# Attention with the next image's keys and queries placed ahead of the last query chunk, and taps in 8-row pieces

## The chip, the core and the metric

The program runs on one NeuronCore of a Trainium2 chip. The metric is the device time of one execution in microseconds (us). Engines are named as the profile names them: PE (TensorE), DVE (VectorE), ACT (ScalarE), POOL (GpSimd), SP (SyncE, which issues the DMAs).

## What is computed

The input is x, 8 images of 64 channels and 128x128 pixels. Layer 0 is an attention over each image, layer 1 a state-space scan over all images. Only layer 0 is touched by the change. For one image, cut to what matters:

```python
x = mean over 2x2 pixels                      # 64 channels, N = 64*64 = 4096 tokens
gap = mean of x over all tokens;  tg = gap * x
q = tg @ Wq.T + bq;  k = tg @ Wk.T + bk
xK = sigmoid(q) * k + tg                      # the keys
y0, y1 = gelu(5-tap depthwise conv of x, vertical / horizontal), 1x1 conv, scale
xQ = Wh @ concat(y0, y1) + bh                 # the queries
xV = x @ Wo.T + bo                            # the values
attn = softmax(xQ @ xK.T / 8);  z = (attn @ xV) @ Wp.T + bp + xV
zn = layernorm(z)                             # 4096 x 64, then upsampled and given to layer 1
```

## The kernel before

`attention_phase` (lines 69 to 618) writes one instruction stream for each engine; semaphores order them. `mamba_phase` follows and is the same in both kernels. An image has N = 4096 tokens; they are cut into NQ = 8 chunks of TB = 512 queries, and the keys into KT = 32 blocks of 128.

**A query chunk** (PE `chunk`, L555; ACT `exps`, L421; DVE `maxima`, L304 and `normalise`, L318). For each of 32 key blocks PE makes scores `st` from `kf` and `qf` in f32 (L565), ACT takes the exponential into `prob` (L433), and PE adds prob times values into `ob` (L580). Softmax needs the row maximum beforehand, so PE also makes bf16 scores `s` of the *next* chunk in 32 blocks (L530, L531, the `ahead` argument), two in each of the first 16 of the 32 steps, and DVE reduces each with a maximum (L308). At step 18 PE turns the maxima into a row (`max_rows`) and ACT writes that row into partition 64 of `qf` at step 20 (L437), where it is subtracted by the score product itself. After the chunk ACT copies `ob` to `osb` (L443); PE projects it at step 3 of the next chunk (L552), DVE normalises it, with a wait for ACT's `rstd` (step 26 of the next chunk).

**The preparation of an image.** POOL adds 2x2 pixels (L241 to L246) as soon as PE has read the old image for the last time (`v_mm`), then makes the horizontal taps over all 64 rows at once: five products (L261) and four sums (L264), each 64x4096. DVE makes the mean (L354) and the vertical taps, `vertical`, chunk by chunk (L298, L301). When an image's eight chunks are over, ACT makes `tg` (L469, L472), then for each chunk PE makes q and k (L592, L593) and the values (L598), ACT the sigmoid (L456) and the bf16 copy `ka` (L459), DVE the keys (L370, L373), the values (L376) and the rest `ka` (L409). After the last of the eight ACT makes eight gelus (L485) with the query products of PE (L606, 128 rows) and the copies `qf`, `qh` (L490, L493) beside them; DVE sets a row of ones (L385) and makes `qm` (L389). Then PE makes the 32 maxima blocks of chunk 0 by themselves, and only then the first chunk starts.

**Order.** All engines loop over the images. DVE's order within an image (`image`, L360) is keys, `maxima` of chunks 0 and 1, then `mean` and `vertical(0)` of the next image, then for each later chunk `maxima`, `normalise`, `vertical`. SP loads the next image's pixels before it stores this image's chunks.

Of the kernel before, what the change touches and what calls it, by code (L numbers as in the profile page):

```python
# [18 lines left out]
ALU = mybir.AluOpType  # L19
# [4 lines left out]
P = 128  # L24
B, C, H, W = 8, 64, 128, 128
HP, WP = H // 2, W // 2
N = HP * WP
# [27 lines left out]
    ("projb", 64, 1), ("lng", 64, 1), ("lnb", 64, 1), ("cent", 64, 64), ("eps", 128, 1),  # L55
# [13 lines left out]
def attention_phase(nc, x, small, sel, zn):  # L69

    with ExitStack() as ctx:
# [9 lines left out]
        wt = sb("a_small", [P, NCOL])  # L81
# [11 lines left out]
        tg = sb("tg", [P, N])  # L93
        kf = sb("kf", [P, N])
        qf = sb("qf", [P, N])
# [3 lines left out]
        v = sb("v", [P, KT, 2 * C])  # L99
# [85 lines left out]

        block = ctx.enter_context(nc.Block())

        @block.sync
        def _(sp):
            sp.dma_start(wt[:, :], small).then_inc(small_in, 16)  # L190
            sp.wait_ge(zeroed, 3)
# [14 lines left out]
            def store_zn(b):  # L206
                with sp.Fori(0, NQ // 2) as j2:
                    for s in range(2):
                        sp.wait_ge(zn_ready[s], b * (NQ // 2) + j2 + 1)
                        dst = zn[bass.ds(HEAD + b * N + (j2 * 2 + s) * TB, TB), :]  # L210
                        sp.dma_start(dst.rearrange("(q p) c -> p q c", p=P),
                                     znb[s][:, :, :]).then_inc(zn_out[s], 16)

            load_x(0, True)
            with sp.Fori(0, B - 1) as b:
                load_x(b + 1, False)
                store_zn(b)
            store_zn(B - 1)
# [5 lines left out]
        def _(pool):  # L224
            pool.memset(zeros[:, :], 0.0).then_inc(zeroed, 1)
            pool.memset(xb[:, :], 0.0).then_inc(zeroed, 1)
            pool.memset(v[:, :, 2 * C - 1:2 * C], 1.0).then_inc(zeroed, 1)
            pool.wait_ge(zeroed, 3)
            with pool.Fori(0, B) as b:

                pool.wait_ge(tap_h, b * 5)
# [17 lines left out]
                yh = yc[64:128, :].rearrange("p (h w) -> p h w", w=WP)  # L249
# [5 lines left out]
                for k in range(5):  # L255
                    tap = dwq[64:128, k:k + 1].unsqueeze(2).broadcast_to([64, HP, WP])

                    to = yh if k == 0 else yg[64:128, :].rearrange("p (h w) -> p h w", w=WP)
                    if k >= 2:
                        pool.wait_ge(tap_h, b * 5 + k)  # L260
                    pool.tensor_tensor(to, xh[:, :, k:k + WP], tap, ALU.mult).then_inc(tap_h if k == 0 else tap_x, 1)  # L261
                    if k > 0:
                        pool.wait_ge(tap_x, b * 4 + k)
                        pool.tensor_tensor(yh, yh, to, ALU.add).then_inc(tap_h, 1)  # L264

        @block.vector
        def _(dve):
# [50 lines left out]
            def normalise(b, j2, s):  # L318

                g = b * NQ + j2 * 2 + s  # L320
# [3 lines left out]
                for qb in range(4):  # L324
                    vq = v[:, bass.ds((j2 * 2 + s) * 4 + qb, 1), 0:C].rearrange("p a c -> p (a c)")
                    dve.scalar_tensor_tensor(z[:, qb, :], zt[:, qb, 0:C], rden[:, qb:qb + 1], vq,
                                             ALU.mult, ALU.add).then_inc(z_step, 1)
# [32 lines left out]
            def image(b, more):  # L360

                for ch in range(NQ):
# [10 lines left out]
                    dve.tensor_tensor(kf[:, cols], kb[:, :], tg[:, cols], ALU.add).then_inc(kf_done, 1)  # L373

                    dve.wait_ge(v_mm, g + 1)
                    dve.tensor_tensor(v[:, ch * 4:ch * 4 + 4, 0:2 * C - 1],  # L376
# [4 lines left out]
                    if ch > 0:  # L381
                        middle(g - 1, ch - 1)
                middle(b * NQ + NQ - 1, NQ - 1)
                dve.wait_ge(ka_done, (b + 1) * NQ)
                dve.memset(kf[64:65, :], 1.0).then_inc(krow, 1)  # L385
                for ch in range(NQ):
                    cols = slice(ch * TB, ch * TB + TB)
                    dve.wait_ge(qh_done, b * NQ + ch + 1)
                    dve.tensor_tensor(qm[:, cols], qf[:, cols], qh[:, cols], ALU.subtract).then_inc(qm_done, 1)  # L389
                maxima(b * NQ)  # L390
                maxima(b * NQ + 1)
                if more:
                    mean(b + 1)
                    vertical(b + 1, 0)
                with dve.Fori(0, NQ // 2 - 1) as j2:
                    for s in range(2):
                        maxima(b * NQ + j2 * 2 + s + 2)
                        normalise(b, j2, s)
                        if more:
                            vertical(b + 1, j2 * 2 + s + 1)  # L400
                if more:
                    vertical(b + 1, NQ - 1)
                normalise(b, NQ // 2 - 1, 0)
                normalise(b, NQ // 2 - 1, 1)

            def middle(g, ch):
                cols = slice(ch * TB, ch * TB + TB)
                dve.wait_ge(kh_done, g + 1)
                dve.tensor_tensor(ka[64:128, cols], kf[64:128, cols], ka[64:128, cols],  # L409
                                  ALU.subtract).then_inc(ka_done, 1)  # L410
# [4 lines left out]
            with dve.Fori(0, B - 1) as b:  # L415
                image(b, True)
            image(B - 1, False)

        @block.scalar
        def _(act):  # L420
            def exps(g, next_cols, rest):  # L421

                for t in range(KT):
                    if t == MAX_ROW_T and next_cols is not None:
                        max_row(g + 1, next_cols)
# [9 lines left out]
            def max_row(g, cols):  # L435
                act.wait_ge(mrow_mm, g + 1)
                act.mul(qf[64:65, cols], rb[0:1, :], -1.0).then_inc(mrow_done, 1)  # L437
# [13 lines left out]
            def keys(b, ch):  # L451
# [5 lines left out]
                if ch > 0:  # L457
                    act.wait_ge(kf_done, g)
                    act.copy(ka[:, (ch - 1) * TB:ch * TB], kf[:, (ch - 1) * TB:ch * TB]).then_inc(kh_done, 1)  # L459

            act.wait_ge(small_in, 16)
            with act.Fori(0, B) as b:
                act.wait_ge(gap_v, b * 3 + 3)
                for ch in range(NQ):
                    g = b * NQ + ch
                    cols = slice(ch * TB, ch * TB + TB)
                    rows = slice(ch * 8, ch * 8 + 8)

                    act.activation(tg[0:64, cols].rearrange("p (h w) -> p h w", w=WP),  # L469
                                   xv[:, 2 + ch * 8:10 + ch * 8, :], ACT.Copy,  # L470
                                   scale=gapf[0:64, :]).then_inc(tg_ready, 1)
                    act.activation(tg[64:128, cols].rearrange("p (h w) -> p h w", w=WP),  # L472
                                   xh[:, rows, 2:2 + WP], ACT.Copy, scale=gapf[64:128, :]).then_inc(tg_ready, 1)
                    if ch > 0:
                        keys(b, ch - 1)
                keys(b, NQ - 1)
                act.wait_ge(kf_done, b * NQ + NQ)
                act.copy(ka[:, N - TB:N], kf[:, N - TB:N]).then_inc(kh_done, 1)
                act.wait_ge(tap_v, (b + 1) * NQ * 5)
                act.wait_ge(tap_h, (b + 1) * 5)  # L480
                act.wait_ge(setup_v, 14)
                for ch in range(NQ + 1):
                    if ch < NQ:
                        cols = slice(ch * TB, ch * TB + TB)
                        act.activation(yg[:, cols], yc[:, cols], ACT.Gelu, bias=w("bdw")).then_inc(gelu_done, 1)  # L485
                    if ch > 0:
                        k = ch - 1
                        cols = slice(k * TB, k * TB + TB)
                        act.wait_ge(ph_mm, b * NQ + k + 1)
                        act.activation(qf[:, cols], s1[k % 2][:, :], ACT.Identity, bias=bqq[:, 0:1])\  # L490
                           .then_inc(qf_done[k % 2], 1)
                        act.wait_ge(qf_done[k % 2], b * (NQ // 2) + k // 2 + 1)
                        act.copy(qh[:, cols], qf[:, cols]).then_inc(qh_done, 1)  # L493
                act.preload_act_table_set(LN_EXP)
                act.wait_ge(qm_done, (b + 1) * NQ)
                max_row(b * NQ, slice(0, TB))
                exps(b * NQ, slice(TB, 2 * TB), False)
                outputs(b * NQ)
                with act.Fori(1, NQ - 1) as j:
                    g = b * NQ + j  # L500
                    exps(g, bass.ds((j + 1) * TB, TB), True)
                    outputs(g)
                g = b * NQ + NQ - 1
                exps(g, None, True)
                outputs(g)
                rstds(g)

        @block.tensor
        def _(pe):
# [15 lines left out]
            def score_block(t, j):  # L525
# [7 lines left out]
            def maxima_blocks(g, j, t):  # L533

                pe.wait_ge(s1_max, g * 32 + t - 1) if t >= 2 else pe.wait_ge(s1_max, g * 32)
                score_block(t, j)
# [798 lines left out]
```

## Time and profile before

| | us |
|---|---|
| median of 3 runs (12467.69 to 12474.12) | 12469.56 |
| the profiled execution | 12465.74 |
| its span, first to last instruction | 12463.9 |
| PE busy in the span | 11440.9 (92%) |
| DVE busy | 9896.2 (79%) |
| ACT busy | 7888.2 (63%) |
| POOL busy | 7860.5 (63%) |

The profiled execution is the one from which all durations here are taken; it lies 3.8 us below the median. The shares are averages over two layers with different limits, so they do not say what bounds the attention. The attention takes the first 4893 us or so; stages of it are read from windows of the trace.

### The profile page before, as it was taken

To read this page: it belongs to the slowest core of one execution; us is meant where nothing else is said; L and a number is where in the kernel's file an instruction comes from. 1 tells how busy PE (TensorE), PEld (TensorE's weight loads), DVE (VectorE), ACT (ScalarE), POOL (GpSimd) and SP (SyncE) were. 2 spreads that over 40 slices of the span, in tenths; PEclk is the share of its full clock that TensorE was granted. 3 is DMA by queue.
4 is the path that set the end of the run, shared out by engine and by line. 5 is a ranking of instruction groups with operands and counts; after the bars stand their busy time and mean duration, and the time that the engine had idled before them with its cause. 6 is when DMAs were issued, how large, how long until landed. Compare 5 with 4: busy or idle time off the path is not lost.

```text
span 12463.9 us, 161217 instructions
## 1 busy us (share of the span) xinstructions
PE 11440.9 (92%) x33768; PEld 4251.5 (34%) x33768; DVE 9896.2 (79%) x12696; ACT 7888.2 (63%) x12821; POOL 7860.5 (63%) x5925
## 2 busy tenths in 40 slices
PE   4989898989899999999999999999999999999998
PEld 1333333333333333333333333333333333333333
DVE  6454545454536344999999999999999999999999
ACT  2333333333333334888888888888888888888888
POOL 6030303030303001999999999999999999999999
PEclk9989898989899999999999999999999999999999
DMA  2010101010100001444444444444444444444444
GB/s 59 2 29 2 28 2 29 2 28 2 29 9 21 3 1 52 174 185 173 180 184 171 183 181 173 185 178 176 185 174 179 185 171 183 182 172 185 179 175 186
DMA packets 408439, 1433.35 MB, mean 115 GB/s; under 512 B 180242, under 2 KB 180370, under 8 KB 267926
## 3 DMA queue, kind: packets, MB, share of 16 engines
q1 hardware_dynamic: 408342, 1432.48, 30.9%
q14 instruction: 88, 0.72, 0.0%
q8 instruction: 9, 0.15, 0.0%
HBM read 1380.68 MB, written 51.62 MB: 115 GB/s over the span
## 4 chain that ended last, share of the span: by engine, by line
DVE 22%; issue 22%; PE 7%; ACT 4%; POOL 3%; DVEq 2%; POOLq 0%; ACTq 0%; DMA 0%; SPq 0%
DVE bbank L940 10%; DVE h L961 9%; POOL e L837 3%; PE vbank L1144 2%; PE vbank L1143 2%; PE ybank L1195 2%; DVE qn L930 1%; ACT L1018 1%; ACT sz L1015 1%; PE ubank L1147 1%; PE bbank L1185 1%; ACT da L1085 1%; ACT so L1053 1%; DVE dl L919 1%; DVE yb L926 1%
## 5 line engine op out<-in xcount | busy, mean ns | idle before, releaser
L871 POOL TENSOR_TENSOR pr<-h,cc 128x512 f32<-128x512 f32 x4109 | 5157.1, 1271 | 543.8 <-DVE h L961 543.6
L961 DVE TENSOR_TENSOR_SCAN h<-da,h,bbank 128x512 f32<-128x512 f32 x3596 | 4497.4, 1261 | 0.0
L1195 PE MATMUL ybank<-pr,m_small 128*128 128x512 f32 x8212 | 4141.5, 595 | 0.3 <-POOL pr L871 0.3
L433 ACT ACTIVATE prob<-st 128x512 f32<-128x512 f32 x2048 | 1222.7, 597 | 2573.5 <-PE st L565 2573.5
L1085 ACT ACTIVATE da<-dl,a 128x512 f32<-128x512 f32 x3599 | 2445.4, 713 | 148.4 <-DVE dl L919 138.4
L940 DVE TENSOR_TENSOR bbank<-bbank,du 128x512 f32<-128x512 f32 x3597 | 2415.7, 672 | 4.4 <-POOL du L841 2.1
L308 DVE TENSOR_REDUCE mpart<-s 128x1 f32<-128x512 f32 x2048 | 1321.4, 686 | 1089.7 <-PE s L531 1081.6
L565 PE MATMUL st<-qf,kf 65*128 (+1 forms) x4096 | 2121.1, 620 | 5.9 <-ACT qf L437 5.9
L241 POOL TENSOR_TENSOR rowsum<-xin 128x1024 f32<-128x1024 f32 x64 | 154.0, 2406 | 2994.2 <-PE vb L598 2905.9
L1185 PE MATMUL bbank<-bcs,selb 96*128 96x512 bf16 x3598 | 1387.3, 386 | 474.4 <-DVE h L961 464.2
L1195 PEld LDWEIGHTS ybank<-pr,m_small 128*128 128x128 f32 x8212 | 1519.4, 191 | 829.7 <-POOL pr L871 378.5
L1185 PEld LDWEIGHTS bbank<-bcs,selb 96*128 96x128 bf16 x3598 | 345.4, 96 | 2192.3 <-DVE h L961 1790.5
L580 PE MATMUL ob<-prob,v 128*64 128x512 f32 x4096 | 1090.6, 616 | 0.0
L565 PEld LDWEIGHTS st<-qf,kf 65*128 65x128 f32 x4096 | 696.3, 190 | 1123.0 <-issue 617.7
L832 POOL TENSOR_TENSOR ed<-ed,av 128x512 f32<-128x512 f32 x258 | 328.7, 1274 | 1034.2 <-ACT ed L1037 1034.2
L530 PE MATMUL s<-ka,qh 128*128 128x512 bf16 x2048 | 791.7, 387 | 132.9 <-DVE mpart L308 109.5
L531 PE MATMUL s<-ka,qm 128*128 128x512 bf16 x2048 | 787.6, 385 | 0.0
L338 DVE TENSOR_SCALAR zn<-z,mv,rstd 128x64 f32<-128x64 f32 x256 | 62.9, 310 | 912.5 <-ACT rstd L449 912.5
L961 DVE TENSOR_TENSOR_SCAN h<-bbank,h,dbp 128x512 f32<-128x512 f32 x513 | 651.9, 1271 | 56.6 <-ACT bbank L1085 56.6
L860 POOL TENSOR_TENSOR dbp<-cc,du 128x512 f32<-128x512 f32 x514 | 653.7, 1272 | 3.3 <-DMA cc<-c_rows 3.3
L1010 ACT ACT_TABLE_LOAD x258 | 331.0, 1283 | 479.2 <-PE vbank L1144 477.0
L301 DVE SCALAR_TENSOR_TENSOR yc<-xb,dwq,yc (+1 forms) x256 | 455.4, 1779 | 33.3 <-DVE yc L301 23.4
(156 smaller groups left out, 12201.2 us busy)
## 6 DMA issues: line engine op xcount, KB each, us to landing
cc<-c_rows SPq DMA_DIRECT2D x1032, 1024.0 KB, 8.0
cc<-c_rows SPq DMA_DIRECT2D x258, 512.0 KB, 11.5
upw<-up SPq DMA_DIRECT2D x260, 256.0 KB, 10.3
xin<-x SPq DMA_DIRECT2D x128, 512.0 KB, 6.7
out<-ot SPq DMA_DIRECT2D x256, 128.0 KB, 2.3
zw<-zn_tokens SPq DMA_DIRECT2D x780, 32.0 KB, 10.5
c_rows<-crows SPq DMA_DIRECT2D x258, 36.0 KB
zn_tokens<-znb SPq DMA_DIRECT2D x64, 128.0 KB, 2.0
```

What stands on the lines that cost most here:

```text
L308: dve.tensor_reduce(mpart[:, t:t + 1], s1[t % 2][:, :], AX.X, ALU.max).then_inc(s1_max, 1)
L433: act.activation(prob[t % 4][:, :], st[t % 2][:, :], ACT.Exp).then_inc(exp_done, 1)
L530: pe.matmul(s1[t % 2][:, :], qh[:, q], keys, start=True, stop=False)
L531: pe.matmul(s1[t % 2][:, :], qm[:, q], keys, start=False, stop=True).then_inc(s1_mm, 1)
L565: pe.matmul(st[t % 2][:, :], kf[0:C + 1, t * P:t * P + P], q, start=True, stop=True).then_inc(st_mm, 1)
L580: mm = pe.matmul(ob[64 * half:64 * half + 64, :], v[:, k + half, C:2 * C], prob[(k + half) % 4][:, :], start=(k == 0), stop=(k == KT - 2))
L871: pool.tensor_tensor(pr[:, n % 8, :], h[:, n, :], cc[par][:, n, :], ALU.mult).then_inc(prod_done, 1)
L940: dve.tensor_tensor(bbank[n % 4][:, :], bbank[n % 4][:, :], du[par][:, :], ALU.mult)\
L961: dve.tensor_tensor_scan(h[:, n, :], decay, inp, h[:, n, TB - 1:TB], ALU.mult, ALU.add).then_inc(scan_done, 1)
L1085: act.activation(to, dl[par][:, :], ACT.Exp, scale=a[:, n:n + 1]).then_inc(da_done, 1)
L1185: pe.matmul(bbank[n % 4][:, :], selb[:, n, :], bcs[par][:, :], start=True, stop=True)\
L1195: pe.matmul(ybank[:, :], w("ident"), pr[:, n % 8, :], start=False, stop=(n == S - 1))\
```

## The change

The image loop is turned by one stage. The keys, values and queries of image b+1 are made between chunk 6 and chunk 7 of image b, and chunk 7 carries the maxima of the next image's chunk 0, which it had none of before. What chunk 7 still reads is kept: two buffers each for the keys (`kt`, which also holds `tg`: the sum is made in place), the values (`vv`) and the last chunk's queries (`qlast`). `tg` is made in chunks 2 to 5, two pieces behind each (`scaled`). All eight gelus come first, then keys and queries chunk by chunk. The query product goes into `ob` instead of `s`. POOL's taps are made in eight pieces of 8 rows (64x512 each). DVE's `mean` comes after the normalising of chunk 0 and the vertical taps follow in chunks 2 to 6, at most two chunks of taps at a time. SP stores six chunks, loads the image after the next, and stores the other two. The load of the small operands leaves out the columns that only layer 1 uses. The last image has no preparation, and its chunk 7 no maxima.

```diff
+        kt = [sb(f"kt{i}", [P, N]) for i in range(2)]
+        qlast = [sb(f"qlast{i}", [P, TB]) for i in range(2)]
+        vv = [sb(f"vv{i}", [P, KT, 2 * C]) for i in range(2)]
...
@block.sync
+            with sp.Fori(0, B - 2) as b:
+                store_zn(b, range(NQ - 2))
+                load_x(b + 2, False)
+                store_zn(b, range(NQ - 2, NQ))
...
@block.gpsimd
+                for ch in range(NQ):
+                    part = slice(ch * TB, ch * TB + TB)
...
+                    for k in range(5):
+                        tap = dwq[64:128, k:k + 1].unsqueeze(2).broadcast_to([64, 8, WP])
...
+                        pool.tensor_tensor(to, xh[:, ch * 8:ch * 8 + 8, k:k + WP], tap, ALU.mult)\
+                            .then_inc(tap_h if k == 0 else tap_x, 1)
+                        if k > 0:
+                            pool.wait_ge(tap_x, (b * NQ + ch) * 4 + k)
+                            pool.tensor_tensor(yh, yh, to, ALU.add).then_inc(tap_h, 1)
...
@block.vector
+            def keys_queries(b, p):
...
                     if ch > 0:
+                        middle(g - 1, p, ch - 1)
+                        query_rest(b, p, ch - 1)
+                middle(b * NQ + NQ - 1, p, NQ - 1)
                 dve.wait_ge(ka_done, (b + 1) * NQ)
                 dve.memset(kf[64:65, :], 1.0).then_inc(krow, 1)
+                query_rest(b, p, NQ - 1)
...
+            def batch(b, p, first, more):
                 maxima(b * NQ + 1)
+                if not first:
+                    normalise(b - 1, 1 - p, NQ - 1)
+                taps = {1: (0, 1), 2: (2, 3), 3: (4, 5), 4: (6,), 5: (7,)}
+                for j in range(NQ - 2):
+                    maxima(b * NQ + j + 2)
+                    normalise(b, p, j)
+                    if more and j == 0:
+                        mean(b + 1)
+                    if more:
+                        for ch in taps.get(j, ()):
+                            vertical(b + 1, ch)
                 if more:
+                    keys_queries(b + 1, 1 - p)
+                    maxima(b * NQ + NQ)
+                normalise(b, p, NQ - 2)
...
@block.scalar
+            def keys_queries(b, p):
+                act.wait_ge(tap_v, (b + 1) * NQ * 5)
+                act.wait_ge(tap_h, (b + 1) * 5 * NQ)
...
+                for ch in range(NQ):
+                    cols = slice(ch * TB, ch * TB + TB)
+                    act.activation(yg[:, cols], yc[:, cols], ACT.Gelu, bias=w("bdw")).then_inc(gelu_done, 1)
+                for ch in range(NQ):
+                    keys(b, p, ch)
+                    cols = slice(ch * TB, ch * TB + TB)
+                    act.wait_ge(ph_mm, b * NQ + ch + 1)
+                    act.activation(queries(p, ch), ob[:, :], ACT.Identity, bias=bqq[:, 0:1])\
+                       .then_inc(qf_done[ch % 2], 1)
+                    act.wait_ge(qf_done[ch % 2], b * (NQ // 2) + ch // 2 + 1)
+                    act.copy(qh[:, cols], queries(p, ch)).then_inc(qh_done, 1)
+                round_keys(b, p, NQ - 1)
+                act.preload_act_table_set(LN_EXP)
...
+                with act.Fori(2, NQ - 2) as j:
+                    exps(b * NQ + j, qf[64:65, bass.ds((j + 1) * TB, TB)], True)
+                    outputs(b * NQ + j)
+                    if more:
+                        for half in range(2):
+                            scaled(1 - p, j * 2 + (half - 4))
+                exps(g + NQ - 2, qlast[p][64:65, :], True)
+                outputs(g + NQ - 2)
+                if more:
+                    keys_queries(b + 1, 1 - p)
+                    act.wait_ge(qm_done, (b + 2) * NQ)
+                exps(g + NQ - 1, qf[64:65, 0:TB] if more else None, True)
+                outputs(g + NQ - 1)
...
@block.tensor
+            def chunk(g, p, q, ahead, behind, fresh=None):
                 pe.wait_ge(mrow_done, g + 1)
+                if fresh is not None:
+                    pe.wait_ge(sig_done, fresh * NQ + NQ)
...
+                    if fresh is not None and t == 1:
+                        pe.wait_ge(qm_done, fresh * NQ + NQ)
+                        pe.wait_ge(krow, fresh + 1)
+                        pe.wait_ge(v_done, fresh * NQ + NQ)
+                    first = 0 if fresh is None else 2
+                    if ahead is not None and first <= t < KT // 2 + first:
...
+            def keys_queries(b, p, behind):
                 for ch in range(NQ):
...
                     mm.then_inc(v_mm, 1)
+                    pe.wait_ge(gelu_done, b * NQ + ch + 1)
...
+                        pe.wait_ge(qf_done[(ch - 1) % 2], b * (NQ // 2) + (ch - 1) // 2 + 1)
+                    pe.matmul(ob[:, :], wc[:, :], yg[:, ch * TB:ch * TB + TB], start=True,
                               stop=True).then_inc(ph_mm, 1)
...
+            with pe.Fori(0, (B - 2) // 2) as b2:
+                for s in range(2):
+                    batch(b2 * 2 + s + 1, 1 - s, False, True)
```

## Rows read from the trace of the kernel before

**Rows 1.** Windows: us, then busy of PE, PEld, DVE, ACT, POOL; PEclk, DMA, GB/s.

```profile
633.70:696.00 62.30, 62.30 (x209) 21.94 (x210) 31.67 (x65) 20.68 (x37) 0.00 (x0) 1.00 0.01 2
696.00:743.30 47.30, 47.29 (x136) 14.91 (x136) 3.77 (x19) 20.05 (x35) 0.00 (x0) 1.00 0.01 3
743.30:839.70 96.40, 74.08 (x192) 32.82 (x192) 62.03 (x96) 41.67 (x64) 33.33 (x22) 0.70 0.40 89
901.90:978.80 76.90, 64.27 (x209) 22.31 (x210) 42.97 (x62) 20.64 (x36) 14.07 (x2) 0.91 0.01 2
```

**Rows 2.** Timeline of ACT: start us, us, engine, line, operation, count, idle before.

```profile
244.98 0.58 ACT L437 ACTIVATE qf<-rb 1x512 f32<-1x512 f32 x1 [25.43 <-PE rb L542]
...
839.68 0.58 ACT L437 ACTIVATE qf<-rb 1x512 f32<-1x512 f32 x1 [25.24 <-PE rb L542]
...
4409.73 0.58 ACT L437 ACTIVATE qf<-rb 1x512 f32<-1x512 f32 x1 [24.60 <-PE rb L542]
```

**Rows 3.** Timeline: POOL and DVE while POOL makes the second image's taps; then PE.

```profile
858.04 8.84 POOL L264 TENSOR_TENSOR yc<-yc,yg 64x4096 f32<-64x4096 f32 x1
...
883.21 33.38 DVE L301 SCALAR_TENSOR_TENSOR yc<-xb,dwq,yc 64x512 f32<-64x512 f32 x4
...
692.82 3.08 DVE L301 SCALAR_TENSOR_TENSOR yc<-xb,dwq,yc 64x512 f32<-64x512 f32 x4
...
917.25 0.61 PE L530 MATMUL s<-ka,qh 128*128 128x512 bf16 x1 [12.63 <-DVE mpart L308]
```

**Rows 4.** Timeline of PE between two images: q and k products of consecutive chunks.

```profile
753.35 2.04 PE L592 MATMUL st<-tg,a_small 64*128 64x512 f32 x2 [8.20 <-ACT tg L472]
...
768.84 1.91 PE L592 MATMUL st<-tg,a_small 64*128 64x512 f32 x2
...
773.96 1.91 PE L592 MATMUL st<-tg,a_small 64*128 64x512 f32 x2
```

**Rows 5.** Windows, columns as in Rows 1: keys, query products (two windows), chunk 1 after its stall.

```profile
760.00:795.00 35.00, 34.65 (x83) 20.51 (x81) 18.66 (x27) 15.53 (x25) 0.00 (x0) 0.50 0.06 14
797.30:801.30 4.00, 3.75 (x4) 1.14 (x4) 3.09 (x3) 2.40 (x5) 3.63 (x4) 0.50 0.00 0
801.50:813.00 11.50, 6.57 (x12) 1.74 (x12) 9.42 (x8) 11.27 (x19) 8.01 (x6) 1.00 0.82 182
917.20:921.00 3.80, 3.75 (x7) 1.36 (x8) 1.97 (x3) 0.12 (x1) 0.00 (x0) 0.50 0.00 0
921.00:925.00 4.00, 4.00 (x22) 2.21 (x20) 2.73 (x5) 1.07 (x2) 0.00 (x0) 1.00 0.01 2
```

**Rows 6.** Groups by line, 743.3 to 839.7 us: busy us, mean ns, idle before.

```profile
L485 ACT ACTIVATE yg<-yc,a_small 128x512 f32<-128x512 f32 x8 | 5.6, 717 | 0.0
L373 DVE TENSOR_TENSOR kf<-kb,tg 128x512 f32<-128x512 f32 x8 | 5.5, 692 | 0.3
L456 ACT ACTIVATE sg<-st,a_small 128x512 f32<-128x512 f32 x8 | 5.5, 687 | 18.4 <-PE st L592 18.4
...
L490 ACT ACTIVATE qf<-s,bqq 128x512 f32<-128x512 f32 x8 | 5.4, 672 | 1.6 <-PE s L606 1.6
...
L493 ACT CAST qh<-qf 128x512 bf16<-128x512 f32 x8 | 4.9, 618 | 0.3
...
L385 DVE MEMSET kf<- 1x4096 f32 x1 | 3.5, 3472 | 0.9 <-DVE ka L409 0.9
...
L469 ACT ACT_TABLE_LOAD x1 | 1.3, 1283 | 2.5 <-issue 2.5
```

**Rows 7.** Timeline of DVE at the end of the keys, POOL busy with the next image.

```profile
795.40 4.31 DVE L409 TENSOR_TENSOR ka<-kf,ka 64x512 bf16<-64x512 f32 x2
```

**Rows 8.** Taps of the first image in POOL's timeline; POOL's 128x512 form on the page.

```profile
66.24 7.01 POOL L261 TENSOR_TENSOR yc<-xb,dwq 64x4096 f32<-64x4096 f32 x1
...
80.58 9.13 POOL L264 TENSOR_TENSOR yc<-yc,yg 64x4096 f32<-64x4096 f32 x1
...
L871 POOL TENSOR_TENSOR pr<-h,cc 128x512 f32<-128x512 f32 x4109 | 5157.1, 1271 | 543.8 <-DVE h L961 543.6
```

More of the change, by code:

```diff
@@ L226, in _ @@
             pool.memset(xb[:, :], 0.0).then_inc(zeroed, 1)
[L227 to L228 removed]
+            for i in range(2):
+                pool.memset(vv[i][:, :, 2 * C - 1:2 * C], 1.0).then_inc(zeroed, 1)
+            pool.wait_ge(zeroed, 4)
             with pool.Fori(0, B) as b:
[L231 removed]
+                pool.wait_ge(tap_h, b * 5 * NQ)
                 pool.wait_ge(v_mm, b * NQ)
@@ L254, in _ @@
                 pool.wait_ge(setup_v, 4)
[L255 to L264, printed above, removed]
+                for ch in range(NQ):
+                    part = slice(ch * TB, ch * TB + TB)
+                    yh = yc[64:128, part].rearrange("p (h w) -> p h w", w=WP)
+                    yx = yg[64:128, part].rearrange("p (h w) -> p h w", w=WP)
+                    for k in range(5):
+                        tap = dwq[64:128, k:k + 1].unsqueeze(2).broadcast_to([64, 8, WP])
+                        to = yh if k == 0 else yx
+                        if k >= 2:
+                            pool.wait_ge(tap_h, (b * NQ + ch) * 5 + k)
+                        pool.tensor_tensor(to, xh[:, ch * 8:ch * 8 + 8, k:k + WP], tap, ALU.mult)\
[3 more added lines that the diff above has]
+                            pool.tensor_tensor(yh, yh, to, ALU.add).then_inc(tap_h, 1)
         @block.vector
@@ L358, in mean @@
                                       ALU.mult).then_inc(gap_v, 1)
-            def image(b, more):
+            def keys_queries(b, p):
+                kf = kt[p]
                 for ch in range(NQ):
@@ L390, in image @@
-                maxima(b * NQ)
-                maxima(b * NQ + 1)
-                if more:
[L393 to L402, printed above, removed]
@@ L414, in _, with exps @@
                 vertical(0, ch)
-            with dve.Fori(0, B - 1) as b:
-                image(b, True)
-            image(B - 1, False)
+            keys_queries(0, 0)
+            maxima(0)
+            batch(0, 0, True, True)
+            with dve.Fori(0, (B - 2) // 2) as b2:
+                for s in range(2):
+                    batch(b2 * 2 + s + 1, 1 - s, False, True)
+            batch(B - 1, 1, False, False)
+            normalise(B - 1, 1, NQ - 1)
         @block.scalar
         def _(act):
-            def exps(g, next_cols, rest):
+            def exps(g, next_row, rest, at=MAX_ROW_T):
                 for t in range(KT):
-                    if t == MAX_ROW_T and next_cols is not None:
-                        max_row(g + 1, next_cols)
+                    if t == at and next_row is not None:
+                        max_row(g + 1, next_row)
                     if t == KT - 6 and rest:
@@ new lines, in _ @@
+            act.wait_ge(small_in, 16)
+            act.wait_ge(gap_v, 3)
+            for ch in range(NQ):
+                scaled(0, ch)
+            keys_queries(0, 0)
+            act.wait_ge(qm_done, NQ)
+            max_row(0, qf[64:65, 0:TB])
+            batch(0, 0, True, True)
+            with act.Fori(0, (B - 2) // 2) as b2:
+                for s in range(2):
+                    batch(b2 * 2 + s + 1, 1 - s, False, True)
+            batch(B - 1, 1, False, False)
+            rstds(B * NQ - 1)
```

199 lines of the change are left out of this document (86 added, 113 removed), and 2 rows, old and new, of the table LAYOUT.

## Prediction

> **What bounds the kernel now.** I read the windows first, stage by stage, because the page's shares mix two layers. In a middle chunk PE is busy for the whole 62.3 us at full clock, with ACT at 20.7 and DVE at 31.7: PE bounds it. Chunk 7, which carries no maxima, takes 47.3. Two stretches fall out of this pattern: the 96.4 us between two images, where PE shows 74 us at a mean clock of 0.70, and chunk 1, which takes 76.9 for the same work [rows 1]. Then the marks on ACT: the first and the last image's first maximum row stand at 244.98 and 4409.73, so a period is 4164.75 / 7 = 594.96 us [rows 2]. Eight chunks of 62.28 (62.30 in the window) would be 498.24; **96.72 us of each period are something else**: 96.4 between images, 14.6 lost in chunk 1 (76.9 less 62.3), less the 15.0 that the short chunk 7 saves [rows 1]; chunk 1 varies a little from image to image.
>
> Why chunk 1 is long: POOL's tap passes last 8.84 us each, and four vertical taps of DVE that take 3.08 by themselves take 33.38 beside them, so the next maxima are late and PE stands for 12.63 us [rows 3]. Why the preparation is slow: after 8.2 us of idle, q to next q is 773.96 - 768.84 = 5.12 us [rows 4], with PE busy 34.65 of 35 us at 0.50, that is 1.2 GHz [rows 5]. So three products (q, k, values) of 5.12 / 3 = 1.71 us each set the pace, and ACT and DVE, at 15.5 and 18.7 of the 35 us, have time to spare.
>
> **The change part by part.**
>
> *Mean and vertical taps move* behind chunk 1, when POOL's taps are long over: POOL starts pooling after the last value product of the stage, ahead of chunk 7, needs some 50 us, then about 105 for the taps (below), and is done early in chunk 1. The 15 us of chunk 1 go. Two chunks of taps take 2 x 4 us after the normalising (3.08 for four of the five instructions [rows 3]); they end about when the next chunk starts, and its first maximum is wanted 1.5 us later: nothing.
>
> *tg moves* into chunks 2 to 5, four copies of 0.72 (as a gelu [rows 6]), about 3.0 us in front of the next chunk's exponentials. PE has two steps (some 3.5 us, from the pace of chunk 1's first steps) before it needs the first of them; ACT is through with it after osb 0.6, the four copies and 0.6 for itself, 4.3 with hops. I take 1.0 us x 4 = **4.0** (0, if PE's steps are slower, to 12, if nothing hides them).
>
> *The stage* stays in line on PE: chunk 7 is issued behind it, so it is not hidden, only rearranged. From the end of chunk 6 [durations: rows 6]:
> 1. osb 0.6, table load 1.28, eight gelus (5.6 busy, overlapping a little) 5.4, table load 1.28, sigmoid 0.69: 9.3.
> 2. keys and values on DVE, three at 0.7 and hops of 0.2: 2.7. Only then may PE write the second chunk's values. PE has nothing to do for 6 us before that, and 8.2 us of idle ended at half clock, so I take half clock from here.
> 3. values and query product of chunk 1: 3.4.
> 4. six turns of q, k, v and query product, 4 x 1.71 = 6.83 us: 41.0. ACT has 2.6 us of work in a turn (sigmoid, ka, qf, qh) and DVE 3.5 (five at 0.7); PE sets it.
> 5. The tail, now in the open: qf 0.67, qh 0.62, ka 0.62, rest of ka 0.69, row of ones 3.47, qm 0.69, six hops 1.2: 8.0. POOL begins to pool beside it; two rests of ka took 4.31 there instead of 1.4 [rows 7], so I add 2.9 once (0 to 6): 10.9.
>
> Sum 67.3, less the 1.1 us (osb and a hop) that lies there in any chunk: **66.2**. Chunk 7 then runs with the maxima, 62.28 (counted). Its start is at half clock: after the stall of chunk 1, PE was at 0.50 for 3.8 us, then at 1.00 [rows 5], so 1.8 lost. The maxima end two steps later, close to the row that uses them: 0.7. The two normalisings beside POOL's taps: 1.0, mostly hidden (0 to 8, below).
> Total 66.2 + 4.0 + 1.8 + 0.7 + 1.0 = 73.7 against 96.72: 23.0 less in each of seven periods, **-161 us**.
>
> *Taps in pieces.* A 64x512 piece is bounded below by an eighth of 7.01 and 8.84 (0.88 and 1.1) [rows 3, 8] and above by POOL's two-tensor 128x512 form, 1.27 [rows 8]; I take 1.03 and 1.25 with hops of 0.1: 90 us an image instead of 72. For images 1 to 7 this hides behind chunks. For the first it does not: DVE gets in between two pieces, which costs POOL 0.3 each time (9.13 against 8.84 [rows 3, 8]), 12 for 40 taps. From 66.24 [rows 8] the taps end at 168; the stage without osb takes 66.7, and the lone maxima of image 0 stay, 25.2 (the idle time before the row at 839.68 [rows 2]): first row at 260 instead of 244.98 [rows 2], **+15**. Bounds: -15 if pieces cost an eighth and DVE fits for nothing, +31 if each costs 1.27 and DVE 0.5.
>
> *Loop ends.* ACT stood 2.5 us with no releaser at the image loop's end [rows 6]; that is in the 96.4, and now the loop runs three times with two images each: **+4** (0 to 8). *Smaller small-operand load, split stores on SP*: nothing; the pixels arrive during chunk 7 and are wanted a period later, and the two stores now queued behind the load wait for POOL's pooling, 50 us from the end of the stage, while the first of them is ready only at the end of chunk 7. On POOL nothing but the next image is queued behind the pieces. On PE the new waits hold all of chunk 7; that is the tail above.
>
> -161 + 15 + 4 = -142: 12465.7 - 142 = 12324 for the profiled execution, 3.8 more for the median: **12327**.
>
> **The rivals.**
> *The clock rises within the stage (0.30).* The rows speak both ways. Dense q, k and v products, 64 rows each, stayed at 0.50 for 35 us; the 128-row query products ended that: four passes at 0.50 up to 801.3, and 1.00 behind them with PE busy only 6.57 of 11.5 us [rows 5]. In the new turn a quarter of PE's time is such a product. At full clock PE needs 3.4 us a turn and DVE's five instructions with hops, 4.2, set it: 2.6 saved in up to six turns of eight stages, -126, so down to 12200. The Trainium skill (TensorE: Matmul & The Clock Gate, Part 1) has it that a PE kept busy is let up to 2.4 GHz; by that rule this rival would hold, and the old keys would have run at 1.00. The measured 0.50 over 35 busy us speaks against the rule for 64-row work, so I hold the other case likelier.
>
> *DVE still waits on POOL (0.08).* POOL's 72 pieces now lie under chunk 7 and chunk 0 instead of chunks 0 and 1. Of two normalisings, twelve instructions could each wait for a piece of 1.27: 15 us a period, of which half has no slack behind it: 7 x 7 = +50, 12377. The Trainium skill (SBUF — State Buffer, Who interferes with whom) lets a DVE instruction with two SBUF inputs and a POOL one that reads SBUF exclude each other for a whole instruction. By that rule the wait would hit them; the taps agree (33.38 against 3.08 [rows 3]), and no row shows a normalising beside POOL.
>
> *Nothing gained (0.03).* A turn is set by the handing over between PE, ACT and DVE and takes 9.0 us: 2.2 more in each of 8 turns of 8 stages, 141, which eats the saving: 12468.
>
> *Slower (0.04): chunk 7 stays at half clock.* Its score products have 65 rows, near those which did not raise the clock. A chunk in which PE is busy throughout takes twice its 62.28 at half: 7 x 60 = +420, some 12750; it decides from 46 us at half clock on (23 lost). Against it: chunk 1 came back in 3.8 us [rows 5], with maxima blocks in it as chunk 7 now has.
>
> **How the numbers follow.** Half clock in the stage 0.55, clock up 0.30, the rest 0.15. The forecast is the likeliest's. Its own range is 12290 to 12365 (first image, POOL's waits, hand-overs). Low end: the clock rises from the second turn on and the first image gains, 12190. High end: DVE waits and the first image at its worst, 12395. A measurement of this kernel can tell about 0.2% (25 us) from no change; the first three cases lie beyond that: faster 0.93, same 0.03, slower 0.04.
>
> **What would show it.** Right: chunk 1 at 62.3 us; period near 572; copies of chunk 6 to first exponential of chunk 7 near 67, with PE at 0.50 and q to q 6.8; chunk 7 near 65; first row near 260. Wrong in a step: q to q near 4.2 (clock); a PE wait on maxima in chunk 0 or 7 (DVE behind POOL); PEclk of 0.50 beyond 5 us of chunk 7; ACT table loads among the exponentials of chunks 2 to 5.

## Result and profile after

The changed kernel takes 12329.1 us (median of 4 runs, 12328.55 to 12330.39) against 12468.76 before (12467.69 to 12474.12): a ratio of 0.9887, 95% interval 0.987 to 0.9904. The profiled execution took 12328.55 with a span of 12326.7, 137.2 less than the one before. The forecast was 12327 with a range of 12190 to 12395.

The page barely moves: PE goes from 11440.9 us of busy time to this (busy us, share of the span, instructions, by engine).

```profile
PE 11430.3 (93%) x33578; PEld 4269.2 (35%) x33768; DVE 9659.4 (78%) x12696; ACT 7881.3 (64%) x12814; POOL 7945.5 (64%) x6430
```

By these records PE lost only 10.6 us of work (190 matmuls fewer are recorded than the chunks and stages issue, so this is rough); most of the gain is idle time that went. To see where, the next rows mark the stages: ACT's timeline (start, us, engine, line, operation, count, idle before) with the gelus' table load in the first image, the first maximum row, the copy `osb` after chunk 0 of the first image, two marks of the second image's stage, and the copy after chunk 0 of the last.

```profile
164.50 1.28 ACT L505 ACT_TABLE_LOAD   x1 [79.87 <-issue]
...
258.77 0.58 ACT L463 ACTIVATE qf<-rb 1x512 f32<-1x512 f32 x1 [31.96 <-PE rb L588]
...
320.97 0.58 ACT L469 COPY osb<-ob 128x512 f32<-128x512 f32 x1 [1.28 <-PE ob L632]
...
1270.61 0.59 ACT L469 COPY osb<-ob 128x512 f32<-128x512 f32 x1 [1.28 <-PE ob L632]
...
1340.06 1.08 ACT L459 ACTIVATE prob<-st 128x512 f32<-128x512 f32 x2 [6.54 <-DVE qm L406]
...
4338.28 0.58 ACT L469 COPY osb<-ob 128x512 f32<-128x512 f32 x1 [1.28 <-PE ob L632]
```

The first row comes at 258.77 instead of 244.98 [rows 2]: 13.8 us **lost** in the first image. From 320.97 to 4338.28 lie seven periods: 573.90 us each instead of 594.96, so 7 x 21.06 = 147.4 **gained**. That is 133.6 in the attention. The last 3.5 lie in layer 1, which is the same code: from the last copy `osb` to the end it took 7570.9 before and 7567.4 here, and 7575.7 in the run with only the taps in pieces, below; it differs by so much between executions.

The 64 copies `osb` cut a period into chunks. Chunk 1 is 62.28 instead of some 77; the four chunks that start behind `tg` copies (3 to 6) are 63.07; chunk 7 with the stage in front of it is 133.5 in the mean (133.85 in the first six, 131.3 in the last, beside which POOL has no further image to pool); two chunk 0, of the fourth and the sixth image, are 66.8, where the image loop jumps back. Windows of a middle chunk (chunk 1 of the third image), the second image's stage, its six turns alone, and chunk 7's start (us, then busy of PE, PEld, DVE, ACT, POOL, with counts; PEclk, DMA, GB/s):

```profile
1466.90:1529.20 62.30, 62.13 (x206) 21.94 (x210) 29.56 (x58) 20.68 (x37) 0.00 (x0) 1.00 0.01 3
1270.60:1342.00 71.40, 59.06 (x118) 28.52 (x119) 35.00 (x41) 30.31 (x46) 9.68 (x6) 0.56 0.15 32
1281.80:1330.10 48.30, 48.30 (x94) 24.23 (x95) 23.94 (x34) 15.01 (x25) 1.05 (x1) 0.50 0.00 0
1342.00:1346.00 4.00, 3.78 (x7) 1.26 (x7) 1.38 (x2) 0.60 (x1) 3.67 (x3) 0.50 0.87 195
1346.00:1350.00 4.00, 4.00 (x19) 2.05 (x18) 1.29 (x2) 0.60 (x1) 3.17 (x3) 0.85 0.49 113
```

In chunk 1 PE is busy for 62.13 of 62.30 us at full clock, as in any middle chunk; in the stage its mean clock is 0.56. The third row is the heart of the stage: PE busy for all of 48.30 us at 0.50, as the old keys were [rows 5]. One turn of it in PE's timeline, q to q:

```profile
1281.76 2.04 PE L651 MATMUL vb<-woq,xb 64*128 64x127 f32 x8 [5.37 <-DVE vv L390]
...
1285.74 2.07 PE L645 MATMUL st<-kt,a_small 64*128 64x512 f32 x2
1287.61 1.91 PE L646 MATMUL s<-kt,a_small 64*128 64x512 f32 x2
1289.31 1.91 PE L651 MATMUL vb<-woq,xb 64*128 64x127 f32 x8
1291.15 2.08 PE L661 MATMUL ob<-yg,wc 128*128 128x512 f32 x2
1293.16 2.07 PE L645 MATMUL st<-kt,a_small 64*128 64x512 f32 x2
...
1330.12 3.62 PE L612 MATMUL st<-qlast,kt 65*128 65x512 f32 x4
1340.71 2.07 PE L612 MATMUL st<-qlast,kt 65*128 65x512 f32 x2 [6.97 <-ACT prob L459]
```

A turn is 1293.16 - 1285.74 = 7.42 us. From start to start, q takes 1.87, k 1.70, the values 1.84 and the query product (128 rows, between products of 64) 2.01. The stage's tail and the normalising beside POOL's pieces, in DVE's timeline:

```profile
1329.08 2.86 DVE L430 TENSOR_TENSOR ka<-kt,ka 64x512 bf16<-64x512 f32 x1
...
1335.75 3.47 DVE L400 MEMSET kt<- 1x4096 f32 x1 [0.91 <-DVE ka L430]
1339.25 0.69 DVE L406 TENSOR_TENSOR qm<-qlast,qh 128x512 bf16<-128x512 f32 x1
...
1395.09 2.66 DVE L351 TENSOR_SCALAR zn<-z,mv,rstd 128x64 f32<-128x64 f32 x4 [10.94 <-ACT rstd L475]
1397.79 1.53 DVE L354 TENSOR_TENSOR zn<-zn,a_small 128x256 f32<-128x256 f32 x1
1399.45 1.05 DVE L359 TENSOR_TENSOR znb<-zn,a_small 128x256 f32<-128x256 f32 x1
...
1406.07 1.29 DVE L320 TENSOR_REDUCE mpart<-s 128x1 f32<-128x512 f32 x2 [5.56 <-PE s L577]
```

Two of POOL's groups by line (busy us, mean ns, idle) are the taps' sums and products of the second to the eighth image (250 to 4900 us):

```profile
L276 POOL TENSOR_TENSOR yc<-yc,yg 64x512 f32<-64x512 f32 x224 | 283.5, 1266 | 17.6
L272 POOL TENSOR_TENSOR yg<-xb,dwq 64x512 f32<-64x512 f32 x224 | 235.3, 1050 | 13.2
```

One rest of `ka` takes 2.86 instead of 0.69 beside POOL's pooling; the row of ones and `qm` keep their 3.47 and 0.69. The normalising is slower beside the pieces (by itself it takes 0.98, 0.43 and 0.43: 3.4 us more), but DVE waits 5.56 us for PE behind it, so it costs nothing.

### The profile page after: what moved, and what is told of

Read it like the earlier page. It is cut to its first block, busy times and chain, and to the rows that moved or that the text cites. A ratio compares the mean times of both kernels' runs of the same rounds, so it can differ in the third digit from the quotient of the medians.

```text
span 12326.7 us, 160391 instructions
## 1 busy us (share of the span) xinstructions
PE 11430.3 (93%) x33578; PEld 4269.2 (35%) x33768; DVE 9659.4 (78%) x12696; ACT 7881.3 (64%) x12814; POOL 7945.5 (64%) x6430
## 4 chain that ended last, share of the span: by engine, by line
DVE 23%; issue 22%; PE 7%; ACT 4%; POOL 3%; DVEq 2%; POOLq 0%; ACTq 0%; DMA 0%; SPq 0%
DVE bbank L1008 11%; DVE h L1029 9%; POOL e L905 3%; PE vbank L1212 2%; PE vbank L1211 2%; PE ybank L1263 2%; DVE qn L998 1%; ACT L1086 1%; ACT sz L1083 1%; PE ubank L1215 1%; PE bbank L1253 1%; ACT da L1153 1%; ACT so L1121 1%; DVE dl L987 1%; DVE yb L994 1%
## 5 line engine op out<-in xcount | busy, mean ns | idle before, releaser
L612 PE MATMUL st<-qf,kt 65*128 (+1 forms) x3584 | 1865.2, 620 | 20.8 <-ACT prob L459 14.6
L632 PE MATMUL ob<-prob,vv 128*64 128x512 f32 x4096 | 1090.5, 616 | 0.0
L612 PEld LDWEIGHTS st<-qf,kt 65*128 65x128 f32 x3584 | 605.8, 189 | 985.3 <-issue 556.6
L576 PE MATMUL s<-ka,qh 128*128 128x512 bf16 x1858 | 709.9, 382 | 2.6 <-DVE mpart L320 2.6
L632 PEld LDWEIGHTS ob<-prob,vv 128*64 128x64 f32 x4096 | 207.9, 134 | 592.3 <-ACT prob L459 536.5
```

Source lines behind the costliest of these rows:

```text
L576: pe.matmul(s1[t % 2][:, :], qh[:, q], keys, start=True, stop=False)
L612: pe.matmul(st[t % 2][:, :], kt[p][0:C + 1, t * P:t * P + P], q, start=True, stop=True).then_inc(st_mm, 1)
L632: mm = pe.matmul(ob[64 * half:64 * half + 64, :], vv[p][:, k + half, C:2 * C], prob[(k + half) % 4][:, :], start=(k == 0), stop=(k == KT - 2))
```

## The experiments

Each diff is cut to the lines that carry the edit.

**1. Which edit removes chunk 1's stall?** Two went with the change: the taps' new place and their cut into pieces. Each was put into the kernel before by itself.

```diff
-                if more:
-                    mean(b + 1)
-                    vertical(b + 1, 0)
...
+                taps = {1: (0, 1), 2: (2, 3), 3: (4, 5), 4: (6,), 5: (7,)}
...
+                    if more and j == 0:
+                        mean(b + 1)
+                    if more:
+                        for ch in taps.get(j, ()):
+                            vertical(b + 1, ch)
```

> The kernel before, with DVE's mean and vertical taps moved behind the normalising of chunk 0 and spread over chunks 2 to 6 as in the changed kernel; nothing else. Theory (chunk 1 is long because DVE sits in a tap behind POOL's 8.8 us passes): chunk 1 falls from 77 to 62.3 in seven images, 7 x 14.9 = 104 less: about 12364, and the time between images stays 96.4. Rival (the turned loop, not the taps, carries the gain): the wait moves to a later chunk, within 25 us of 12469.

Measured: 12360.91, ratio 0.9914 (0.9898 to 0.9931). Chunk 1 is 62.28 in all images; the rest is as before.

```diff
+                for ch in range(NQ):
+                    part = slice(ch * TB, ch * TB + TB)
...
+                            pool.tensor_tensor(yh, yh, to, ALU.add).then_inc(tap_h, 1)
```

> The kernel before, with only POOL's taps cut into 64x512 pieces. Theory: a vertical tap waits for one piece of 1.3 us instead of a pass of 8.8, five of them take some 10 us and end before the first maxima of chunk 1 are wanted, so chunk 1 is 62.3: -104. In the first image DVE's taps end near 132 us instead of 165, the keys follow, and the first row comes near 213 instead of 245: -32. Together about 12333, as fast as the changed kernel with its turned loop. Rival (the turned loop carries the gain): pieces still block DVE in chunk 1 or lengthen POOL's work, 12440 to 12480.

Measured: 12328.05, ratio 0.9888 (0.9871 to 0.9904): **as fast as the whole change**, with the image loop unturned. In its timeline, the first maximum row on ACT, then DVE's taps and maxima beside POOL's pieces:

```profile
214.62 0.59 ACT L441 ACTIVATE qf<-rb 1x512 f32<-1x512 f32 x1 [25.69 <-PE rb L546]
...
836.35 1.08 DVE L302 TENSOR_SCALAR yc<-xb,dwq 64x512 f32<-64x512 f32 x1
837.47 6.21 DVE L305 SCALAR_TENSOR_TENSOR yc<-xb,dwq,yc 64x512 f32<-64x512 f32 x4
858.29 1.29 DVE L312 TENSOR_REDUCE mpart<-s 128x1 f32<-128x512 f32 x2 [14.61 <-PE s L535]
```

Four vertical taps take 6.21 instead of 33.38 [rows 3], and it is now DVE that waits 14.61 us for PE. Either edit alone takes the stall away. Only the pieces also help the first image: its row comes at 214.62 instead of 244.98 [rows 2], in the first edit at 245.72.

The period of the pieces alone is 580.1 us ((4337.74 - 276.82) / 7 between the copies after chunk 0). So turning the loop is worth 580.1 - 573.9 = 6.2 x 7 = 43 us, and it gives back 258.8 - 214.6 = 44 in the first image: there, keys now come behind the gelus, which wait for all taps, where before keys were made while the taps ran.

**2. The other way round: whole passes in the turned loop.**

```diff
-                for ch in range(NQ):
-                    part = slice(ch * TB, ch * TB + TB)
...
+                for k in range(5):
+                    tap = dwq[64:128, k:k + 1].unsqueeze(2).broadcast_to([64, HP, WP])
```

> The changed kernel with POOL's taps again in whole passes of 64x4096 (8.8 us). Theory (a normalising that falls beside POOL's taps waits for a pass with each instruction that has two SBUF inputs or runs in the fast mode): the normalisings in chunk 7 and chunk 0 take up to 50 us instead of 2, the next maxima are late, chunk 0 or 1 grows by 20 to 40 us in seven images: 12470 to 12610, with a PE wait on maxima. The first image: taps end near 165 as with pieces. Rival (normalising does not meet the taps, only the old place of the vertical taps did): no chunk grows, 12315 to 12335.

Measured: 12447.2 (one run), 118 above the change. Chunk 0 grows to 82 to 84 us in six images. DVE's timeline in one of them, from 1420 us on (so the first line has three of its four operations), then the wait of PE there (waiter, releaser; us, count, longest):

```profile
1419.89 7.46 DVE L347 TENSOR_SCALAR zn<-z,mv,rstd 128x64 f32<-128x64 f32 x3
1427.38 8.91 DVE L350 TENSOR_TENSOR zn<-zn,a_small 128x256 f32<-128x256 f32 x1
1436.43 7.13 DVE L355 TENSOR_TENSOR znb<-zn,a_small 128x256 f32<-128x256 f32 x1
```

```profile
PE s L572 <- DVE mpart L316: 17.9, 1, 17.9
```

One product of the normalising takes 8.91 us, a whole pass of POOL (8.84 [rows 3]), instead of 1.53 beside pieces, and PE waits 17.9 for the maxima behind it. So the pieces are what makes the turned order possible; with whole passes the stall only moves from chunk 1 to chunk 0. The theory had the direction right and the size too large. The Trainium skill (SBUF — State Buffer, Who interferes with whom) says of such a pair of DVE and POOL instructions that one locks the other out for its whole length; this row agrees, where the trace before had no normalising beside POOL.

The first image's first maximum row in this run, in ACT's timeline, comes as late as with pieces (258.77):

```profile
257.63 0.59 ACT L459 ACTIVATE qf<-rb 1x512 f32<-1x512 f32 x1 [31.52 <-PE rb L584]
```

**3. Does the number of rows hold the clock down in the stage?** The products of q, k and values were given 128 rows instead of 64, with zeros in the lower half of the weights: the columns and the sums stay the same.

```diff
-        woq = sb("woq", [64, 2 * C - 1])
+        woq = sb("woq", [P, 2 * C - 1])
...
+            dve.memset(woq[64:128, :], 0.0)
...
-                    pe.matmul(st[ch % 2][:, :], w("wqT"), kt[p][0:64, cols], start=True, stop=True).then_inc(q_mm, 1)
+                    pe.matmul(st[ch % 2][:, :], full("wqT"), kt[p][:, cols], start=True, stop=True).then_inc(q_mm, 1)
```

> The changed kernel with the q, k and value products made on all 128 rows: the weights' lower 64 rows are zero, so the sums are the same and the columns streamed are the same. Theory (64-row work, however dense, does not bring the clock up): PE goes to 1.00 within some 10 us of the stage, a turn falls from 7.4 to 4.2 to 5 us (set by DVE), 12 to 18 us less in each of eight stages and chunk 7 starts warm: 12170 to 12240. Rival (what keeps the clock down is the waits between the products, not their rows): PEclk stays 0.50 in the stage and the turn at 6.8 to 7.4: 12300 to 12335; it falls to 6.8 if the 0.6 beyond four products is the change between 64 and 128 rows.

Measured: **12146.61**, ratio 0.9743 (0.9727 to 0.976). Windows of the second image's stage, columns as above, then PE's timeline: the last query product at half clock, two turns, and chunk 7:

```profile
1236.70:1240.50 3.80, 3.78 (x11) 2.77 (x12) 2.86 (x5) 0.09 (x1) 0.00 (x0) 0.50 0.00 0
1240.50:1262.00 21.50, 21.50 (x86) 12.50 (x86) 19.38 (x29) 14.97 (x25) 0.74 (x1) 1.00 0.00 1
```

```profile
1238.56 1.92 PE L663 MATMUL ob<-yg,wc 128*128 128x512 f32 x2
1240.27 1.17 PE L647 MATMUL st<-kt,a_small 128*128 128x512 f32 x2
...
1243.88 1.02 PE L647 MATMUL st<-kt,a_small 128*128 128x512 f32 x2
...
1247.35 1.02 PE L647 MATMUL st<-kt,a_small 128*128 128x512 f32 x2
...
1272.93 2.07 PE L614 MATMUL st<-qlast,kt 65*128 65x512 f32 x2 [9.82 <-ACT prob L461]
```

After 3.8 us at 0.50 the granted clock is 1.00, and a turn takes 3.47 us instead of 7.42. PE busy throughout was not enough: the same products on 64 rows stayed at 0.50 for 48.3 busy us. The stage with chunk 7 is some 111 us instead of 133.5 (7 x 22.7 = 159), and the first row comes at 236.40 (22 earlier); together 181 of the 182.5 gained. It went below the theory's range, since DVE, busy 19.38 of 21.5 us, still keeps up with PE at 3.47 a turn. The tail is now the longest wait: PE stands for 9.82 us behind chunk 7's first two blocks of scores. At half clock, too, a product is shorter where its neighbours have 128 rows: the query product takes 1240.27 - 1238.56 = 1.71 us from its start to the next, against 2.01 between products of 64 rows.

The same edit in the unturned kernel of experiment 1 with the pieces:

> The kernel before with two edits: taps in pieces, and q, k and value products on 128 rows; the image loop is not turned. Theory (the clock is what the old preparation lost; the turned loop is worth little by itself): a turn of the keys falls from 5.1 us to about 3 (DVE's four instructions), 8 turns of 8 images, 135 less than pieces alone: 12180 to 12210. The difference to the changed kernel with 128 rows (12147) is then what turning the loop is worth once the clock is up, 35 to 60. Rival (turning the loop is worth nothing even then): 12140 to 12155. Rival (the clock stays down here, since the stage starts after 8 us of idle): 12320 to 12335.

Measured: 12223.68, ratio 0.9801 (0.9784 to 0.9819), 104 less than the pieces alone, and 14 above the theory's range. Its keys in windows:

```profile
706.00:710.00 4.00, 2.22 (x3) 1.17 (x4) 0.00 (x0) 3.02 (x6) 0.00 (x0) 0.50 0.77 169
...
714.00:718.00 4.00, 4.00 (x18) 2.33 (x17) 2.62 (x5) 3.44 (x6) 0.00 (x0) 1.00 0.68 145
```

So at half clock the turned loop is worth nothing over the pieces (12329.1 against 12328.05), and at full clock 77 us (12146.61 against 12223.68). By the traces, the seven periods gain 7 x 13.14 = 92 at full clock (551.14 against 564.28) where they gained 43 at half clock, and the first image gives back 22 (236.40 against 214.59) instead of 44; the other 7 lie in layer 1, the same code. The clock helps the new order more: it takes 3.95 us off a turn, which holds the query product too, but only 2.29 off a turn of the old order (5.12 to 2.83).

**4. The smaller terms.** Each run undoes one of the costs that the forecast listed.

The row of ones made chunk by chunk, ahead of the tail:

```diff
                         query_rest(b, p, ch - 1)
+                        ones(b, p, ch - 1)
...
-                dve.wait_ge(ka_done, (b + 1) * NQ)
-                dve.memset(kf[64:65, :], 1.0).then_inc(krow, 1)
```

> The changed kernel with the row of ones written chunk by chunk (1x512, eight times) behind each chunk's rest of the query, instead of once (1x4096) at the end of the stage. Theory (the tail of the stage is a chain on DVE, and 3.5 us of ones with the 0.9 us in front are part of it): first exponential of chunk 7 some 4.4 us sooner in eight stages, 35 less: about 12294. Rival (the tail is held by POOL's pooling, which DVE meets whatever it does): no more than 10 less, 12318 to 12330.

Measured: 12310.08 (ratio 0.9871, 0.9853 to 0.9888), in between: 19 us. In the trace a period falls by 3.09 (573.90 to 570.81), of the 3.47 that the memset takes. The tail in DVE's timeline:

```profile
1323.87 2.86 DVE L434 TENSOR_TENSOR ka<-kt,ka 64x512 bf16<-64x512 f32 x1
...
1329.66 2.72 DVE L410 TENSOR_TENSOR qm<-qlast,qh 128x512 bf16<-128x512 f32 x1
```

The rest of `ka` takes 2.86 as before, but the last `qm` now 2.72 instead of 0.69: without the memset ahead of it, it falls beside POOL's pooling, which takes part of the gain back.

The `tg` copies between the exponentials instead of behind them:

```diff
-                    if more:
-                        for half in range(2):
-                            scaled(1 - p, j * 2 + (half - 4))
+                    exps(b * NQ + j, qf[64:65, bass.ds((j + 1) * TB, TB)], True, after=after)
```

> The changed kernel with the four copies of tg put between exponentials of the second half of the chunk (after steps 21, 23, 27, 29), where ACT waits for PE 1.5 us in every two steps, instead of behind the chunk. Theory (the 0.79 us that chunks 3 to 6 grew are these copies in front of the next chunk's exponentials): chunks 3 to 6 go back to 62.28, 7 x 4 x 0.79 = 22 less: about 12307. Rival (ACT's gap is too short for a copy of 0.72 with its hops): the copies delay exponentials, 12325 to 12360.

Measured: 12309.43, ratio 0.9869 (0.9852 to 0.9887). All four chunks are back at 62.28: the copies' cost was 0.79 x 4 x 7 = 22 us.

The image loop written out on PE, ACT and DVE:

```diff
-            with pe.Fori(0, (B - 2) // 2) as b2:
+            for b2 in range((B - 2) // 2):
```

> The changed kernel with the loop over pairs of images written out on PE, ACT and DVE. Theory (the two periods in which chunk 0 took 66.8 instead of 62.3 are the loop's two jumps back): both fall to 62.3, 9 less: about 12320. Rival (they come from elsewhere, such as the order of stores and loads): no change, 12326 to 12331; or longer, where more code has to be fetched.

Measured: 12323.32, ratio 0.9881 (0.9863 to 0.9898). Both chunks of 66.8 are 62.28.

The first image's keys ahead of its gelus, as in the kernel before:

```diff
+                if apart:
+                    for ch in range(NQ):
+                        keys(b, p, ch)
+                    round_keys(b, p, NQ - 1)
                 act.wait_ge(tap_v, (b + 1) * NQ * 5)
```

> The changed kernel with one difference in the first image alone: its keys and values are made before its gelus and queries, while POOL still makes the taps (the old order), instead of side by side behind the last tap. Theory (the 43 us that the turned loop gains in seven periods are given back in the first image, where nothing runs beside the preparation): first row near 215 instead of 258.8, as with pieces in the old loop, so 12285 to 12295. Rival (the first image is held by POOL's taps and the lone maxima in either order): 12315 to 12330.

Measured: 12293.73, ratio 0.986 (0.9844 to 0.9876), 35 less. The first row in ACT's timeline shows where it came from, 222.98 against 258.77:

```profile
222.98 0.58 ACT L465 ACTIVATE qf<-rb 1x512 f32<-1x512 f32 x1 [24.96 <-PE rb L602]
```

**5. Together.** Products on 128 rows, `tg` between the exponentials, the loop written out (on POOL too), and the row of ones by POOL, chunk by chunk, ahead of its pooling (DVE also makes the last `qm` ahead of the last rest of `ka`):

```diff
+                for ch in range(NQ):
+                    pool.wait_ge(ka_done, b * NQ + ch + 1)
+                    pool.memset(kt[b % 2][64:65, ch * TB:ch * TB + TB], 1.0).then_inc(krow, 1)
```

> The changed kernel with q, k, values on 128 rows, tg inside the chunk, the image pairs written out, and the row of ones made by POOL chunk by chunk ahead of its pooling, so that neither the ones nor the pooling lies beside DVE's tail. Theory (the costs are separate): from 12147, -22 for tg, -6 for the loop, and the tail from 11 us to 4 or 5, 6 less in eight stages, -48, with some more where chunk 7 starts warm: 12055 to 12080. Rival (with the clock up the tail is held elsewhere, by ACT's copies or the table load): 12100 to 12120.

Measured: 12059.89, ratio 0.9672 (0.9656 to 0.9688). The stage with chunk 7 falls from 111 to 103.3. A window of chunk 7's start shows what is left there, the clock below full again:

```profile
1249.00:1253.00 4.00, 4.00 (x13) 1.76 (x11) 1.94 (x3) 0.60 (x1) 3.79 (x3) 0.60 0.18 27
```

With the first image's keys ahead of its gelus as well (the edits of both runs):

> The kernel of e11_all with the first image's keys and values made before its gelus, as in e10_first_apart. Theory: with the clock up the side by side stage is shorter, so less is given back in the first image than in e10_first_apart: 20 to 30 less than e11_all. Rival (no gain, since with the clock up the order does not matter): within 8 of e11_all.

Measured: **12053.08**, ratio 0.9666 (0.965 to 0.9683), the fastest of all: 276 us below the change and 415 below the kernel before. The last edit is worth 7 here and 35 by itself: the 20 to 30 expected did not come, and the rival held. Once the clock is up, the first image's keys behind its taps are short. The first row stands at 223.52, no earlier than without the full clock (222.98), since POOL's taps hold it in both. The table load ahead of the first gelu waits for the last of them, here and in the run with only the first image changed:

```profile
170.59 1.28 ACT L537 ACT_TABLE_LOAD   x1 [14.38 <-POOL yc L286]
```

```profile
170.80 1.28 ACT L519 ACT_TABLE_LOAD   x1 [3.66 <-POOL yc L276]
```

## Why the prediction was right, and where it was off

The total holds: -142 was forecast for the profiled execution and -137.2 measured. Half clock, the case taken at 0.55, is what happened. Point by point:

- *Chunk 1's stall goes*: right, 62.28. The text gave the new place of the taps as the reason. The runs show that the pieces alone do it too, and that in the new order the place needs the pieces.
- *The stage, 67.3*: measured 69.45, from 1270.61 to 1340.06. To the sigmoid's end 8.9 (9.3), to the second values 2.25 (2.7), to the next q 3.98 (3.4), six turns 1330.12 - 1285.74 = 44.4 (41.0), tail 9.94 (10.9). **The term that failed is the turn**: "4 x 1.71 = 6.83" priced all four products as the old three [rows 4], and it took 7.42. The extra 0.6 lies at the change between products of 64 and of 128 rows: in the run where all have 128 rows, the query product takes 1.71 at the same half clock instead of 2.01, and four products take 3.47 at full clock, twice which is 6.94. A whole turn without the change was not measured at half clock.
- *The tail*: POOL beside it costs 133.85 - 131.3 = 2.5, against 2.9.
- *Chunk 7's start*: the second image's stage with chunk 7 takes 133.98. A chunk is 62.28 of it and the stage without its `osb` 68.35 (69.45 - 1.1), so 3.3 is lost, against 1.8 + 0.7 (and 1.0 for the normalising, which cost nothing). PE stayed below full clock until after 1346.
- *`tg` copies*: 0.79 a chunk for 1.0. *Loop ends*: two jumps of 4.5, 9 for 4.
- *First image*: +13.8 for +15, with taps that ended at 164.5 for 168 (pieces of 1.05 and 1.27 us in the later images, for 1.03 and 1.25). The sum puts the whole stage behind the taps, which is what happened. But +15 and its bounds were told as the price of slower taps on POOL. That was the wrong cause: with whole passes in the turned loop the row is as late, at 257.63, and the pieces alone brought it *forward* by 30 us. The later row comes from the keys' place behind the gelus, worth 35 in its own run.

Summed: the periods gave 147.4 where 161 less the loop's 4, or 157, was forecast, 9.6 short: 5 from the loop, the rest from the turn's 7 x 3.4 = 24 less what most other terms of the stage came out cheaper. The first image came 1.2 cheaper and layer 1 varied by 3.5, which leaves 4.9, the difference of 142 and 137.2. So it is in part luck that the median lies within 2 us of the forecast: the errors nearly cancel.

Of the rivals: the clock did not rise, and the third experiment shows that the 64 rows kept it down, as the forecast held likelier. The price of that rival was too small: in that run the clock rose and 12146.61 was measured, below the range's 12190, since DVE's five instructions take 3.47 us a turn and not 4.2. By the rule of the Trainium skill (TensorE: Matmul & The Clock Gate, Part 1), that a PE kept busy goes to full speed, 48.3 busy us at 0.50 should not occur. The measurement decides: the same products went to 1.00 on 128 rows, so in this kernel the rows count. Normalising beside POOL waited, 3.4 us, but inside DVE's slack. Chunk 7, whose products go on at 1340.71, stood at 0.50 to 1346 and at 0.85 in the 4 us behind that: a little beyond the 5 us named as a sign, but it did not stay at half. Hand-overs did not set the turn: PE was busy throughout.

What the forecast missed is not in its total: the whole gain could have been had with the pieces alone, and the larger part of the change paid 44 us in the first image for 43 in the periods.

## What to carry to other kernels

When a change has several edits, price each by itself against the kernel before: a cheap one (cut the long instructions of an engine that blocks another) can hold all of the gain, and a costly reordering may pay for itself only once another limit is lifted. Moving a stage by one iteration charges the first iteration as well; look there for what was hidden and now is not. Where dense products on few rows (64 of 128 here) run at a granted clock of 0.50, try filling the rows with zeros before anything is rearranged around them.

## What had not been expected of the hardware

- Padding the contraction from 64 to 128 rows with zero weights halved the time of the same products (7.42 to 3.47 us a turn), because the granted clock went from 0.50 to 1.00 after 3.8 us. Whether the rows read or the weights loaded count was not separated.
- At half clock, four products alternating between 64 and 128 rows took 0.6 us more than four of one kind were priced at. The 128-row product took 2.01 us between products of 64 rows and 1.71 between products of 128.
- A jump back of the image loop cost 4.5 us, in the chunk behind it.
- Vertical taps of DVE beside POOL's 64x512 pieces took 1.55 us each, against 8.3 beside whole passes [rows 3] and 0.77 alone.
